# Five engines' written-out orders re-made: the same steps of an attention chain, interleaved anew

## What is computed

```
L0: z = norm(x); x = x + mha(z, ctx)                    8 heads of 32
    u = norm(x);  x = u + program and bias row;  h_t = state recurrence over 1024 tokens (silu)
    x = x + h @ Cmat
L1: x = x + mha(norm(x), norm(ctx))                     16 heads of 64, causal mask in the first tile
L2: x = norm(x + mha(x, ctx)) * g + b                   16 heads of 16, mask multiplied
L3: x = x + mha(norm(x), norm(ctx))                     16 heads of 16, masked
    x = x + fc2(gelu(fc1(norm(x))))                     256 -> 1024 -> 256
```

## Time and profile before

| | |
|---|---|
| median of 3 runs | 1275.66 us (1275.61, 1275.66, 1278.7) |
| the profiled execution: its time / its span | 1278.7 us / 1277.0 us |
| tensor (PE) busy | 1244.4 us, 97% of the span |
| vector (DVE), scalar (ACT), gpsimd (POOL) busy | 923.4, 724.8, 567.4 us |
| chain that ended last | PE 80%, DVE 10%, POOL 4%, ACT 4% |

### The profile page before, as it was taken

The page is one execution under the profiler, slowest core; times in us unless marked ns, Lnnn a source line. Parts: engine busy times, 40 slices in busy tenths (PEclk is TensorE's granted clock), DMA queues, the critical chain, the costliest instruction groups (busy, mean ns, idle before and its releaser), DMA issues.

```text
span 1277.0 us, 24759 instructions
## 1 busy us (share of the span) xinstructions
PE 1244.4 (97%) x9539; PEld 1028.1 (81%) x9539; DVE 923.4 (72%) x1916; ACT 724.8 (57%) x1583; POOL 567.4 (44%) x697
## 2 busy tenths in 40 slices
PE   7999998999999999999999999999999999999998
PEld 6899997777787788888887887788888887788777
DVE  4777773688677777777777557777777777777873
ACT  4677775524655556655555433565555555556574
POOL 4455433015545545364454312554445454454552
PEclk9999999999999999999999999999999999999999
DMA  4523214030000000000000100000000000000000
GB/s 118 121 80 102 61 34 145 1 97 1 9 1 2 2 22 18 13 5 1 1 9 14 50 1 14 15 9 18 1 18 9 14 1 22 2 1 1 14 1 22
DMA packets 48470, 34.21 MB, mean 27 GB/s; under 512 B 22177, under 2 KB 45536, under 8 KB 48352
## 3 DMA queue, kind: packets, MB, share of 16 engines
q1 hardware_dynamic: 48304, 32.59, 9.3%
q10 hardware_dynamic: 48, 0.01, 0.0%
HBM read 23.26 MB, written 8.39 MB: 25 GB/s over the span
## 4 chain that ended last, share of the span: by engine, by line
PE 80%; DVE 10%; POOL 4%; ACT 4%; issue 1%; DMA 1%; SPq 0%; DVEq 0%; POOLq 0%
PE ps L914 10%; PE ps L853 9%; PE ps L879 9%; PE ps L988 8%; PE ps L977 7%; PE ps L863 6%; PE ps L937 6%; PE ps L821 6%; PE ps L921 5%; PE ps L804 4%; PE ps L910 2%; PE ps L1084 2%; DVE mx L1409 2%; DVE zt L1387 1%; PE ps L888 1%
## 5 line engine op out<-in xcount | busy, mean ns | idle before, releaser
L1639 POOL TENSOR_TENSOR rstd<-mv,halfneg 128x1 f32<-128x1 f32 x192 | 105.7, 553 | 362.5 <-DVE mv L1378 361.7
L853 PE MATMUL ps<-wk,tt 128*128 128x308 f32 x512 | 145.0, 424 | 0.0
L977 PEld LDWEIGHTS ps<-tt,fc 128*128 128x128 f32 x1024 | 117.6, 192 | 11.0 <-ACT tt L1183 8.0
L1466 DVE TENSOR_TENSOR xt<-xt,ps 128x256 f32<-128x256 f32 x160 | 66.0, 414 | 81.6 <-PE ps L937 39.1
L1678 POOL TENSOR_TENSOR front<-mx,front 128x616 f32<-128x616 f32 x64 | 80.8, 1263 | 97.0 <-DVE mx L1409 96.8
L977 PE MATMUL ps<-tt,fc 128*128 128x128 f32 x1024 | 123.2, 278 | 0.0
L1678 POOL TENSOR_TENSOR pr<-mx,pr 128x616 f32<-128x616 f32 x64 | 81.0, 1265 | 91.3 <-DVE mx L1409 90.7
L1207 ACT ACTIVATE pr<-pr 128x616 f32<-128x616 f32 x128 | 91.3, 715 | 48.6 <-POOL pr L1678 27.0
L853 PEld LDWEIGHTS ps<-wk,tt 128*128 128x128 f32 x512 | 93.0, 190 | 30.4 <-issue 2.8
L1214 ACT ACTIVATE pr<-ps 128x640 f32<-128x640 f32 x128 | 89.8, 707 | 47.3 <-PE ps L879 39.4
L1183 ACT ACTIVATE tt<-ps,cols 128x128 f32<-128x128 f32 x192 | 77.1, 455 | 67.0 <-PE ps L804 66.5
(11 more groups left out here) (223 smaller groups left out, 2905.9 us busy)
## 6 DMA issues: line engine op xcount, KB each, us to landing
out_dram<-xt SPq DMA_DIRECT2D x64, 128.0 KB, 1.8
xt<-in_x_dram SPq DMA_DIRECT2D x32, 128.0 KB, 2.4
xt<-out_dram SPq DMA_DIRECT2D x32, 128.0 KB, 2.2
fc<-in_L_xattn_fc_w_dram SPq DMA_DIRECT2D x2, 1024.0 KB, 8.1
wk<-in_L_xattn_wkv_dram SPq DMA_DIRECT2D x4, 512.0 KB, 6.6
front<-in_L_xattn_wkv_dram SPq DMA_DIRECT2D x4, 512.0 KB, 5.4
wo<-in_L_xattn_wo_dram SPq DMA_DIRECT2D x1, 1024.0 KB, 6.3
kb<-in_L_xattn_wq_dram SPq DMA_DIRECT2D x1, 1024.0 KB, 6.3
```

The source lines that it names most:

```text
L853: last = mm(bank(lane, k)[:, SFROM[k]:SFROM[k] + HB * KEYS], t[:, lane, kc, :], wk[:, kc, b, h0:h0 + HB * KEYS], start=kc == 0, stop=kc == ...
L977: last = mm(bank(lane, c // 4)[:, c % 4 * P:(c % 4 + 1) * P], fc1[:, kc, c * P:(c + 1) * P], t[:, lane, kc, :], start=kc == 0, stop=kc == ...
L1639: p.tensor_tensor(rstd[:, n:n + 1], mv[:, n, 1:2], halfneg[:, :], ALU.pow).then_inc(done["rstd"], 1)
```

## The change

Only `TURNS` changes: all five strings are replaced. No step is added or removed, no instruction, buffer or wait changes; only the order in which each engine takes the steps of different lists does. Compared by position, 637 of 1428 steps stand elsewhere on `tensor`, 1257 of 1879 on `vector`, 551 of 1106 on `scalar`, 460 of 649 on `gpsimd` and 160 of 176 on `sync`, mostly by a few places. The two strings of an engine can be decoded by hand; what the prediction uses of them is:

| engine | before | after |
|---|---|---|
| tensor, set-up | ... `item_mm 12` (position 16), `query` lane 2 | `query` lane 1, `item_mm 12` (position 17) |
| tensor, recurrence | `scan_mm 2`, `wqt_mm 4`, `scan_mm 3`, ... | `wqt_mm 4`, `scan_mm 2`, `wqt_mm 5`, `scan_mm 3`, ... |
| tensor, recurrence | `scan_mm 16`, `wk_mm 002`, `scan_mm 17`, `wk_mm 010` | `wk_mm 002`, `scan_mm 16`, `wk_mm 010`, `scan_mm 17` |
| tensor, first run of phase 2 | `query 2` lane 2, `pturn 2.1` lane 1 | swapped |
| tensor, run 10 | `scores 3.1`, `pturn 1.0` lane 1, `fc2 ma` | `fc2 ma`, `pturn 2.0` lane 0, `pturn 1.0` lane 1 |
| tensor, last runs | `fc2 ma` lane 1 run 15 at position 1410 | at 1404, six steps earlier |
| scalar | `exp` and `gelu` alternate: 64 changes of table | 68 changes of table |
| sync, start | three `load`s of run 1, `v0_put 0`, one `weights_get`, the fourth `load` | `v0_put 0`, two `weights_get`s, `load` lane 2 run 1, five `weights_get`s, `load`s lanes 0 and 3, three `weights_get`s, `load` lane 1 |
| sync, next | `v0_put 1`, `put` lane 0, two `weights_get`s, `load` lane 0 run 2 | `v0_put 1`, four `weights_get`s, `put` lane 0, `load` lane 0 run 2 |
| sync, end of phase 1 | `weights_get 32` (1 MB), `put`s, `wkv1_get 00`, `get` lane 3, `put`, `wkv1_get 01`, `02`, `03` | `weights_get 32` some 10 `load`s and `put`s earlier; `wkv1_get 00`, three `put`s, `01`, two `put`s and three `get`s, `02`, `03` |
| gpsimd, end of phase 1 | `vtw_zero 0`, `keep u` lane 2 run 7 | `keep u` lane 2 run 7, `keep u` lane 1 run 7, `vtw_zero 0` |

```
 TURNS = {
     "tensor": (
-        "iiiiiiii021ii0iii2ii1i21iii0iiii2i1ii0ii0i1321030301202302132013012001301301310230120322312031303121200210323103"
...
-        "130210322013023310321023012013213021102302103120323310321032021301321021130132322332310203123aaaaaaaaaaaasassasa"
-        "sasasaasaasaasaasaasaasaasaasasasasasasasaasasaasaasasaasaasasasaasasaasaaaa0aaaaa301012103213020102010102101312"
...
-        "1203103302133131012012302300202s13102103003012320221023103113120213211011130230233210312202130230322312210201300"
-        "2302133132013010333320123121102123023002103101002013200223123013031132102132110110320231332310220201203221302220"
...
-        "2012030020213101002020023123123013031132102132110111302303321302102202313203223102221031003202133131020310332333"
-        "120121103120320020302100312312321323231013011212323213332121223233132132323332323333"),
+        "iiiiiiii012ii0ii1ii2ii0iii2ii1ii0ii2ii1i2i0310230130120312013103203102301030103210123022312312031230132302100301"
...
+        "031203101302231302320120123010321312102302102130212310332031230031023110132132322332301213023aaaaaaaaaaaasasasas"
+        "asasasaasaasasaasaasaasaasaasasaasasasasaasasasaasasasaasaasasasaasasaasaaaa0aaaaa031012103213020102010102101312"
...
+        "1020310303213133011231203200202131021003031203120220123031131202132111101302303321302122021302303222013221301003"
+        "202133132013010332s333120121102123023002103101003202002312312031031131202132101102303211233012320201203232103220"
...
+        "0321320020213101020320023212013013031131202132101111302302332130102202313203223221021301002302133131020310330213"
+        "332012311201320020302100312312321323231031012123213233132112132232332132323332323333"),
     "vector": (
...
     "scalar": (
-        "iiiiiii0i12ii210iiii21i0i021301302303210012031100132302102133300212103321210031322023110323120013320211310022320"
...
-        "1323223310230213aaaaaaaaaasaasassssaasaassaaaasasaaasaasaasaasaassssssssssssssssssssssssssssssssss01130021002101"
...
+        "iiiiiii0i211i02iiiii02ii1021303210301321003021130012302102331232100313022130013212012303122301103320121310032201"
...
+        "1323223301230123aaaaaaasaasaasassaasasaasaasaasaaasaasaasasaasaassssssssssssssssssssssssssssssssss01130200012101"
...
     "gpsimd": (
-        "ii201iii01320021020311123320003310a112213322003301201112332203030a1120122133323001102332121023300110201312232330"
-        "0110233122103100132233a20012330120100011110000022220021111101222132001313332220103333200030313220000133011112003"
...
+        "i0i12iii13200122000111332323000311a2230132a130302110022133122033010102222131330301120130322133201100012232331203"
+        "01200121132332100323321a0110320000011112100030022222001111102302122100133322231133330120003303220000303111210133"
...
     "sync": (
-        "1123030aa2aaaaaaaaaaaaa0aa01aa12aa332a0012a1a3230a0112a3aaa2300112323aa00a1a3132201210332a2a33a31aaa000213b1022b"
-        "1aaa000113212302213233101b01b022b330b101233120021033212332110023"),
+        "aa2a201aaaaa033aaa1aaaaaaaa00211a3a23001a1223300aaa1221aa033011a323aaa2a00a1122a33a01022133301a023a22133aaa01a1a"
+        "020b13b102231230320100bb01131b2220331b32221100200231133231012033"),
 }
```

More of the change, by code:

```diff
@@ new lines @@
+        "202133132013010332s333120121102123023002103101003202002312312031031131202132101102303211233012320201203232103220"
+        "210301301231203313101032330123231211021232032301010230120212303123100113b123b2132131112b3bbbbb3bb33bb2bb2bbbb3bb"
+        "bbbbbbbbbbbb22bbbb2bbbbb3bbb3b3bbb3b2b02120212021023130200130203010101310130010332303010320120113012320020131021"
+        "0030021302312201230311312021321101123013033210321022023132032213022213010032102331310203103333321021021103123020"
+        "2013102100123020022132130112301323013211213021103203213231020130230322122201301002301321331302031033320133210211"
@@ new lines @@
+        "0321320020213101020320023212013013031131202132101111302302332130102202313203223221021301002302133131020310330213"
+        "332012311201320020302100312312321323231031012123213233132112132232332132323332323333"),
+    "vector": (
+        "i00ii131022132iiii002ii2ii11iii223i00201100011323121022100001333321113233003200320001103113100220122333312211232"
+        "3110020323203030301111122000012122331211331332320022200030113313110011202220022221233333111322030003333011002122"
+        "1131231022301300333231121222000033311010011102211033200323221233211320032211003330011222111001220200331133212332"
+        "3320203331111112230300022233323sssssssssssssssasassasasasassaassasaaasaaaassaassaasaaasssaasaaa0a0a0aa0aa1111330"
+        "2322023110000010101011122101322222222310000310111003033310230000131100203221200010121203100111220000021222211122"
+        "0001200110103111310000000330222233331111123023233313132320222011300311102211132300320231030000230020331313221102"
+        "0222211110323303311111002011133000002233333223331212001110220021312222002212131131003320002031002213321130132333"
+        "2313321322221000301113101311202320320321300000223003303321121122220032231103031123010101112211310300020233333332"
+        "2122130100012011132222002212311131000030230002333322210112121333233222323030001101000311113111302232020003210033"
+        "02323313131122022212220010101233310111133210121223030002023233231133332112222113120212111133233212332332bbbbbb33"
+        "bbb3bbbb32bbb32b32bb3b3b222bbbbb2bb3b3bbbb3b30000111123002221120000000032111311112021203000100333003120210001022"
+        "0010232100033011013320011111331101002003232333211333020112120121030222220022121311103030030000221132221333201133"
+        "3233113323022202110011133031132122203020310003002300203133132220011222233120300111033211011133110120200032233131"
+        "3322121321322202120000122321101011330332200003222000213131321130233331133222320011311100312110023300232233100000"
+        "2002301333132221221002210233031103013201111133101212002002333332332122301002121010131222220120131131000002330001"
+        "2313222113322130333311332302222003031113110111332222203000130000223000333311212102220102223330111300302111113310"
+        "121000203322333333212221312112223213123232133213311212322333323233222323233333313333023"),
```

49 lines of the change are left out of this document (14 added, 35 removed).

## The result

The new order is slower: 1286.4 us (median of 4 runs, 1285.27 to 1286.94) against 1277.02 for the kernel before on the same chip, ratio 1.0072, 95% interval 1.0054 to 1.009. I had forecast 1273.1 us, within 1265 to 1283. The profiled execution took 1289.58 us, its span is 1287.9: it is 2.6 us longer than the slowest of the four, so its rows show where the time goes better than how much.

A forecast was written before the change was run, and what follows sets the result against it. It took PE, busy 1244.4 of 1277.0 us in a nearly full queue, as the bound. Terms -1.6 - 0.8 - 1.0 + 0.8 + 0 + 0 = -2.6 us off the 1275.66 us median gave 1273.1 us, range 1265 to 1283.

The forecast's parts named there:

- Together +0.8 us, between 0 and 8: Start of the sync queue: lateness of lane 0's second tile, 0.5 us, and its run 2 load, 0.3 us.
- the first case: Lane 0's second tile of `x` lands at 39.1 us after the usual 2.4 us, at a cost of 0.
- goes out at about 54 and lands at 56.5: `load` of lane 0 run 2, wanted by DVE at about 56.7 us: just in time, 0.3 us, bounds 0 and 3.
- The weights of L1: -1.6: At `k_mm 010`, start of L1: weights land before PE asks, removing a 1.63 us wait; all or nothing.
- the recurrence: -1.8: Recurrence: 0.8 us gained at `scan_mm 2` and 1.0 us at the other `carry` waits; bounds 0 and 2.5.
- the 1.5 that I gave: Sign in the profile after: waits of L1099 for `carry` (L1531) in the recurrence under 1.5 us in sum.
- Swaps in phase 2: net 0, within 7 either way: Phase 2: up to 1.8 us of waits removed, 1.4 us new in the tail, elsewhere new waits like the old.
- three waits that I took as removed: Phase 2: lane 2's `query` 0.47 us, lane 1's `pturn 1.0` 0.76 us, the tail's `proj 2` 0.54 us.
- 1.4 us that I counted in the tail: Tail: new wait between `proj 3` and `turn m` of lane 2, whose norm `fc2 ma` no longer covers.
- Table loads: 0: ACT: four more table changes, 5.1 us of ACT time, taken as covered; 5.1 us the upper bound.
- B: Rival at the start: second tiles of `x` come late, up to 8 us, net +4.6, about 1280 us; chance 0.12.
- C: Rival: phase 2 gets worse by 7 us, table loads included, net +4.4, about 1280 us; chance 0.15.

The follow-up runs named there:

- new_again: The new kernel measured again, unchanged: 1285.92 us, ratio 1.0074, 9.9 us over the kernel before.
- start_only: New order up to about 62 us on all five engines, the old order behind it: 1280.23 us, ratio 1.0033 to the kernel before.
- queue_old: The new kernel with the first 32 entries of the sync order as before, all compute orders new: 1281.67 us, ratio 1.0044 to the kernel before.
- start_old: Old order on all five engines up to about 62 us, the new order from there: 1282.34 us, ratio 1.0053 to the kernel before.
- queue_start: The kernel before with only the first 32 entries of the sync order from the new kernel: 1279.29 us, ratio 1.0022.
- middle_only: The kernel before with the new order from about 147 to 262 us on all engines: 1273.31 us, ratio 0.998.
- phase1_old: Old order up to about 147 us on all engines, the new order behind it: 1279.03 us, ratio 1.0026 to the kernel before.
- rows_behind: The new kernel with four mask loads behind lane 0's third tile and three row loads behind lane 2's sixth: 1283.69 us, ratio 1.0064.
- queue_middle: The kernel before with only sync entries 76 to 112 in the new sequence, compute orders old: 1276.13 us, ratio 1.0001.
- new_560_860: The kernel before with the new order from about 147 to 262 us and about 560 to 860 us: 1277.29 us, ratio 1.001.
- tables_back: The new kernel with lane 1's `gelu mb` of runs 8 and 10 right behind `gelu ma`, 64 table changes instead of 68: 1288.75 us, ratio 1.0106.
- mix_best: `middle_only` plus two phase 2 stretches in the new order, about 856 to 886 and 1050 to 1100 us: 1273.74 us, ratio 0.9977.
- masks_last: The new kernel with the four mask loads behind the loads of lane 0's and lane 1's third tile: 1287.73 us, ratio 1.0093.
- middle_compute: The kernel before with the new order of the four compute engines from about 147 to 262 us, sync order old: 1278.6 us, ratio 1.0017.
- phase2_old: New order up to about 262 us, the old order of phase 2 behind it: 1280.45 us, ratio 1.0036 to the kernel before.

## Why the prediction was wrong, point by point

I had summed to -2.6 us, and the new kernel is 9.9 us over the kernel before (`new_again`): the start +3.2 to 4.2 where I had +0.8, 62 to 147 us +2.5 to 3.3 where I had nothing, the middle -2.4 where I had -3.4, phase 2 +5.1 to 5.9 where I had 0.

**The step that failed first: "Together +0.8 us, between 0 and 8", for the first queue positions.** The term is 3.2 to 4.2 us (4.2 by `start_only`, 4.0 by `queue_old`, 3.2 by `start_old`), and the queue alone makes 3.2 (`queue_start`). What I said of lane 0's second tile held: it landed by 38.4 us and cost PE 0.26 us of idle (0.42 in `new_again`), near the first case. What failed is the sentence on the `load` of lane 0 run 2: "goes out at about 54 and lands at 56.5. That is just in time". In the five traces that have the new start unchanged it goes out at 54.85, 55.05, 55.27, 56.18 and, in the profile of the kernel after, 57.49. That is 1 to 3.5 us late. In the first three of them the larger part of the error is when the tile is wanted. I took 56.7 us from the profile of the kernel before, and that execution had a fall of the clock to half from 28 to 32 us, which I had not looked for. In `middle_only`, with the same start and no such fall, the pair of `stats` that was at 56.36 is at 54.31, of which 0.4 us is there already at `v0_put 0`. In the five traces of the new start DVE was free for the tile at 54.7 to 55.7 us. So the tile was 2.0 to 2.5 us late in four of them, and 4.2 in the profile of the kernel after, where I had it in time; and no term stood for the fall of the clock behind such an idle.

The addends were off too. Over the old 49.47 us I added 1 + 1.2 + 2.4 = 4.6 us, for a late queue, two more masks and the landing of the `put`. `new_again` has 0.3 + 3.1 + 2.0 = 5.4 and the profile of the kernel after 2.7 + 3.1 + 2.2 = 8.0. All four masks, not two, now stand ahead of the `put`; the `put` itself stood ahead of the `load` before, so only what its landing takes more counts (4.0 and 4.2 us instead of 2.0). And `v0_put 0` begins at 20.82 us against 20.83: my 0.7 us for `item_mm 12` came to nothing.

**What had no term: 62 to 147 us, 3.3 us.** I followed the queue to 57 us and took the rest of phase 1 as free, because PE idled only 1.6 us there before. It was free because the old queue was just in time everywhere. I had not followed the later loads at all. Over their own befores `queue_old` and `phase1_old` differ by 2.5 us, so the stretch is 2.5 to 3.3 us, if the start's compute orders cost nothing. Part of it may be the 128 KB row loads (`rows_behind`, not settled); that their neighbours are the rest is argued from the waits for tiles in `start_old`, not shown.

**The weights of L1: -1.6, and the recurrence: -1.8.** The sum of the two was 3.4 and the middle gains 2.4 us. The split was wrong in kind: I counted the wait for the weights as theirs alone, and `queue_middle` shows that removing it is worth nothing, since `wqT` was ready only 0.35 us before them. In the kernel after the signs held: `k_mm 010` has no DMA wait, and L1099's waits fell to 1.0 us (under the 1.5 that I gave). But there everything is late; with the old start, 0.48 to 1.70 us of DMA wait stay in four of the five kernels with the new middle. `k_mm 010` started at 223 us instead of by 216 us, because everything was some 7.6 us late by then.

**Swaps in phase 2: net 0, within 7 either way.** It is +5.1 to +5.9 us, the largest of the terms that I had wrong. It lies inside the bounds, and the middle of them was no estimate: "new waits of the same size and number as the old" had no row behind it. Of the three waits that I took as removed, two are gone and have a new one a few steps on, and the third is still there, 0.60 us at `proj 2` (the row at 1249.64 us above) where it was 0.54. The two new ones, in the kernel after, behind the `query` of lane 2 and at the second half of lane 1's `pturn 1`:

```profile
319.47 0.44 PE L888 MATMUL ps<-ident,zt 128*128 128x128 f32 x2 [0.80 <-ACT zt L1219]
...
523.75 0.77 PE L879 MATMUL ps<-ident,front 128*128 128x128 f32 x5 [0.56 <-DVE front L1445]
```

No single place makes it: sampled every 20 us against `middle_only`, the lateness rises by 0.2 us or more in 19 samples, by 1.1 at most, and falls in 10, by 1.3 at most; the slice from 560 to 860 us alone makes 3.4 us (`new_560_860`). The largest single wait of the new order there, in the kernel after:

```profile
830.43 0.44 PE L804 MATMUL ps<-ident,zt 128*128 128x128 f32 x2 [1.41 <-DVE zt L1387]
```

It answers to a wait of 0.81 us in the old one. The 1.4 us that I counted in the tail are there: from 1240 us to the end of the kernel after seven waits sum to 3.75 us, and in `middle_only` six, from 1233 us, to 2.13 us. I had counted them and then let them vanish in "net 0".

**Table loads: 0.** Nothing in `tables_back` speaks against it, but it shows the loads together with a changed order, so they are not priced alone. Of the kernel after, with the columns of the earlier trace rows:

```profile
L1207 ACT ACT_TABLE_LOAD x33 | 42.3, 1283 | 0.6
```

**The rivals.** B (0.12) and C (0.15) were both true at once. I had set each against the gain alone, +4.6 and +4.4 us, and drew the upper end at 1283; the ends of both terms together, by my own bounds, are 1275.7 - 3.4 + 8 + 7 = 1287. Treating independent losses as alternatives is what made the range too narrow. That 1287 would have held the result is partly luck: some 3 us of the loss, from 62 to 147 us, had no term in it.

## What to carry to other kernels

When PE idles less than 2% and the profile shows almost no waits in a stretch, that says nothing of how far its inputs are from being late: before a queue is reordered, follow every load in the stretch with the landing times that hold behind its new neighbours, not with the median. Look, too, whether the execution from which due times are read lost time to the clock. Price a removed wait only after looking what was hidden behind it (here `wqT`, ready only 0.35 us earlier), and test a reorder of queue and compute as a pair as well as apart. When one order is spliced into another at a cut, count the joins: the middle's gain carried over, those of `mix_best` did not. The version to keep is `middle_only`: 1273.31 us, ratio 0.998 to the kernel before and 1% under the new one.

## What the runs showed of the hardware

**Half clock behind an idle stretch.** In nine of these traces the granted clock fell to 0.50, the 1.2 GHz level, at the end of an idle stretch of PE or just behind it: of 3.72 us in the kernel after (6.8 us long), and (some 3.4 us each) of 3.69 in `masks_last`, 2.63 in `queue_start`, 2.32 in `middle_compute`, 2.07 in `phase2_old`, 1.85 in `start_only`, 1.70 in `middle_only`, 1.66 in `new_again` and 1.53 in `tables_back`. From `middle_only`:

```profile
214.00:216.00 2.00, 1.19 (x7) 1.23 (x8) 0.00 (x0) 0.00 (x0) 0.00 (x0) 0.83 1.05 370
216.00:218.00 2.00, 2.00 (x10) 2.00 (x10) 0.38 (x1) 1.12 (x5) 0.00 (x0) 0.50 0.27 91
```

As an estimate from the halved clock each such fall costs half its length, 1.7 to 3.4 us. `middle_only` bears it out: around `k_mm 010` it falls 2.8 us behind `mix_best`, which has the same order there, and its longer wait (1.70 us against 0.51) makes only 1.2 of them. The mean clock of an execution tells of it without a trace: all 11 executions of `start_only` and all 5 of `new_again` have 0.999, all 9 of `phase1_old` and all 5 of `queue_old` 1.000. An idle stretch is neither enough nor needed: 1.83 us at 41.6 us in `queue_start` and 2.22 us at 607 us in `tables_back` had none behind them, and the traces of the kernel before, `queue_middle` and `middle_compute` have a fall from 28 to 32 us with hardly any idle ahead.

**A thousand microseconds to within one.** With the same order of phase 2, nine executions agree over 1005 us to 0.8 us, and seven of them to 0.4, while their first 250 us differ by 2 us and more.
